# Three mixtures of experts routed by tiles of one expert, with results sent to the tokens' rows

## The reference

```python
# layer 0: two experts a token; h has 512 columns, even ones gate, odd ones linear
t = x * rsqrt(mean(x*x) + 1e-5) * norm_scale
top_v, top_i = top_k(t @ gate_w + gate_b, 2);  probs = softmax(top_v)
h = swiglu(t @ w1[e] + b1[e]);  y = h @ w2[e] + b2[e]      # 128 -> 512 -> 256 -> 128
out = x + sum over e of w[:, e] * y
# layer 2: two experts a token, weights taken from the softmax over all eight
h = gelu(x @ W1[e] + b1[e]);  y = h @ W2[e] + b2[e]         # 128 -> 512 -> 128
# layer 3: one expert a token, the one with the nearest centroid
xn = rms_norm(x) * scale;  a, g = split(xn @ up_w[e])
y = (a * silu(g)) @ down_w[e];  out = y + x                  # 128 -> 512 -> 256 -> 128
```

## Time and profile before

| | us |
|---|---|
| median of 3 runs (lowest, highest) | 4087.44 (4083.16, 4087.86) |
| the profiled execution | 4092.16 |
| its span, first to last instruction | 4090.2 |
| busy in the span: PE, DVE, ACT, POOL | 3379.1, 2559.2, 2091.9, 1303.2 |

### The profile page before, as it was taken

The page is one execution under the profiler, slowest core; times in us unless marked ns, Lnnn a source line. Parts: engine busy times, 40 slices in busy tenths (PEclk is TensorE's granted clock), DMA queues, the critical chain, the costliest instruction groups (busy, mean ns, idle before and its releaser), DMA issues. The chain is left out here.

```text
span 4090.2 us, 79250 instructions
## 1 busy us (share of the span) xinstructions
PE 3379.1 (83%) x30561; PEld 2308.1 (56%) x30561; DVE 2559.2 (63%) x6887; ACT 2091.9 (51%) x3789; POOL 1303.2 (32%) x893
## 2 busy tenths in 40 slices
PE   2999999788999879898999998565468999979742
PEld 1677776556566556664555555343345777656542
DVE  6788888556788679676565554698453222269623
ACT  2677776444555547555555554544175444447521
POOL 3554544122222225203455544232120000015344
PEclk8999999999999989899999999777788999989777
DMA  4333333121000010000000000000420000000012
GB/s 124 53 57 54 53 56 50 51 83 42 1 1 1 1 58 2 1 1 1 2 2 2 2 2 2 6 19 24 135 74 7 1 1 1 1 32 2 5 44 65
DMA packets 74212, 114.31 MB, mean 28 GB/s; under 512 B 19692, under 2 KB 56766, under 8 KB 72446
## 3 DMA queue, kind: packets, MB, share of 16 engines
q1 hardware_dynamic: 71356, 104.89, 10.5%
q0 software_dynamic: 2048, 4.20, 0.4%
q10 hardware_dynamic: 434, 0.15, 0.0%
HBM read 62.45 MB, written 30.47 MB: 23 GB/s over the span
## 5 line engine op out<-in xcount | busy, mean ns | idle before, releaser
L856 PE MATMUL banks<-XT,weight_region 128*128 128x512 f32 x1184 | 549.2, 600 | 1.4 <-DVE T L1231 1.4
L878 PEld LDWEIGHTS banks<-weight_region,HT 128*128 128x128 f32 x3648 | 437.1, 192 | 98.5 <-issue 79.9
L878 PE MATMUL banks<-weight_region,HT 128*128 128x128 f32 x3648 | 442.2, 275 | 6.4 <-ACT HT L1013 5.9
L1254 DVE SCALAR_TENSOR_TENSOR x_res<-banks,WT,x_res 128x128 f32<-128x128 f32 x544 | 153.0, 344 | 405.1 <-PE banks L878 365.8
L856 PEld LDWEIGHTS banks<-XT,weight_region 128*128 128x128 f32 x1184 | 212.7, 193 | 194.2 <-issue 191.4
L1008 ACT ACTIVATE HT<-banks,weight_region 128x512 f32<-128x512 f32 x256 | 173.3, 687 | 239.7 <-PE banks L856 233.5
L458 DVE TENSOR_REDUCE MX<-banks 128x8 f32<-128x1152 f32 x128 | 173.2, 1353 | 103.7 <-PE banks L275 103.6
L1071 POOL TENSOR_TENSOR FNM<-FNM,FRS 128x8 f32<-128x8 f32 x12 | 2.4, 203 | 666.6 <-ACT FRS L967 666.6
L2284 POOL TENSOR_TENSOR SM<-SM,RZ 128x1232 f32<-128x1232 f32 x64 | 143.9, 2249 | 188.4 <-DVE RZ L2326 187.3
L384 ACT COPY PT<-banks 128x384 f32<-128x384 f32 x384 | 170.3, 478 | 48.9 <-PE banks L285 45.0
L285 PE MATMUL banks<-sb_c_ident,SM 128*128 128x128 f32 x1152 | 183.3, 286 | 9.8 <-ACT PT L384 9.4
(11 more groups left out here) (550 smaller groups left out, 8403.7 us busy)
## 6 DMA issues: line engine op xcount, KB each, us to landing
FL<-RAW SPq DMA_DIRECT2D x512, 64.0 KB, 2.3
sorted_rows<-in_zeros_dram SPq DMA_DIRECT2D x33, 512.0 KB, 8.2
T<-s4d_k_dram SPq DMA_DIRECT2D x8, 1024.0 KB, 9.3
weight_region<-in_l_ffn__w_dram SPq DMA_DIRECT2D x3, 2048.0 KB
film_dram<-F SPq DMA_DIRECT2D x8, 512.0 KB, 2.9
FO<-film_dram SPq DMA_DIRECT2D x8, 512.0 KB, 4.3
weight_region<-in_l_ffn__wall_dram SPq DMA_DIRECT2D x1, 3072.0 KB, 10.2
XR<-sorted_rows SPq DMA_DIRECT2D x39, 64.0 KB, 1.8
```

The source lines that it names most:

```text
L856: nc.tensor.matmul(PS[:, q % 4, :], w, xt, start=True, stop=True).then_inc(s.h_ps, 1)
L878: ins = nc.tensor.matmul(PS[:, 4 + u % 2, b * P:(b + 1) * P], HT[:, u % 2, j, b * P:(b + 1) * P], w2[j], start=j == 0, stop=j == len(w2) - 1)
L1254: ins = nc.vector.scalar_tensor_tensor(R[:, t, :], PS[:, 4 + u % 2, b * P:(b + 1) * P], WT[:, t, e:e + 1], R[:, t, :], ALU.mult, ALU.add)
```

## The change

`l0_ffn` and `l2_ffn` now call `routed` too, with two rows a token (K = 2); `l3_ffn` keeps K = 1. `routed` itself is rewritten in these places:

- The number of tiles is 71 for K = 2 and 39 for K = 1. All of them always run.
- A row in `sorted_rows` has 132 numbers instead of 128: the token, the number of its row in the result buffer, and its weight. ScalarE writes these rows into `SRC`, once for each choice (`source`). GpSimd scatters 64 times 128 rows for K = 2, 32 times for K = 1.
- Eight row buffers (LD), and four for staged weights (WB). A register load fetches eight table entries at once (`held`), on SP and on each engine that copies weights.
- Who copies weights: ScalarE all 768 numbers in `l3_ffn`; ScalarE 516 and GpSimd 256 in `l0_ffn`; GpSimd 516 and VectorE 512 in `l2_ffn`.
- The result of a tile is multiplied by the row's weight as it is copied out, and one `DMA_INDIRECT` of GpSimd (`send`) scatters its 128 rows to the tokens' rows in `expert_results`; padding rows go to dummy rows. VectorE works out where (`destination`). SP stores nothing in the loop.
- The bias of the second product no longer enters in the tile loop; it is added to `x_res` in the front (`spread`, `bias`, `base`).
- The tail has no gathers. SP waits for all sends, then loads eight groups of results in token order with plain DMAs (512 KB each for K = 2, 256 KB for K = 1). For K = 2 GpSimd adds the two results of a token, then VectorE adds to `x_res`.
- In the front the rank products of a pair (`ranks`) come before the logits of the next pair; before, they came after.
- The buffer of sorted rows is zeroed as before, in rows of 132.

```diff
+ROW = 132
+RESULTS = 2 * ROWS + (2 * B_ALL + 8) * P
...
+    LD, WB, ST, HELD = 8, 4, 4, 8
+    FAR = float(1 << 20)
+    copies = {"gated": {"act": (0, STAGED)}, "gelu": {"pool": (0, FIRST), "dve": (FIRST, STAGED)},
+              "swiglu": {"act": (0, FIRST), "pool": (FIRST, STAGED)}}[kind]
...
+        def held(eng, table, j, top):
+            n = min(HELD, NT - j)
+            regs = [eng.alloc_register(f"held{nc.next_id()}") for _ in range(n)]
+            eng.load(regs, table[0:1, j:j + n])
+            return [eng.snap(r, donate=True, min_val=0, max_val=top) for r in regs]
+
+        def expert(e, part):
+            return W.wall.rearrange("p e n -> p (e n)")[:, bass.ds(e * STAGED + part[0], part[1] - part[0])]
...
+                sp.wait_ge(s.tab, 1)
+                at = held(nc.sync, RWI, 0, SORTED - P)
+                sp.wait_ge(E.moved, MOVED + 16 * K * NB)
+                for j in range(NT):
+                    if j >= LD:
+                        sp.wait_ge(s.t_ps, j - LD + 1)
+                        sp.wait_ge(s.dst, j - LD + 1)
+                        if K == 2:
+                            sp.wait_ge(s.y_sb, j - LD + 1)
+                    sp.dma_start(XR[:, j % LD, :], rows[bass.ds(at[j % HELD], P), :]).then_inc(loads[j % LD], 16)
+                    if (j + 1) % HELD == 0 and j + 1 < NT:
+                        at = held(nc.sync, RWI, j + 1, SORTED - P)
+                for o in range(ST):
+                    sent(sp, o, len(range(o, NT, ST)))
+                took = results[0:K * ROWS].rearrange("(k p t) d -> p k (t d)", k=K, p=P)
+                for g in range(NG):
+                    sp.dma_start(G[:, g], took[:, :, g * GT:(g + 1) * GT]).then_inc(fetched[g], 16)
...
-                def fetch(j):
-                    if j >= LD:
-                        sp.wait_ge(s.t_ps, j - LD + 1)
-                    r = nc.sync.value_load(ROWI[0:1, j:j + 1], min_val=0, max_val=SORTED - P)
-                    sp.dma_start(XR[:, j % LD, :], rows[bass.ds(r, P), :]).then_inc(loads[j % LD], 16)
-
-                def put(j):
-                    r = nc.sync.value_load(ROWI[0:1, j:j + 1], min_val=0, max_val=SORTED - P)
-                    sp.wait_ge(s.y_sb, j + 1)
-                    sp.dma_start(rows[bass.ds(r, P), :], Y[:, j % ST, :]).then_inc(stores[j % ST], 16)
-
-                sp.wait_ge(s.tab, 1)
-                sp.wait_ge(E.moved, 16 * KTOP * NB)
-                for j in range(NT + LEAD):
-                    if j < NT:
-                        fetch(j)
-                    if j >= LEAD:
-                        put(j - LEAD)
...
+                def rows_out(j):
+                    act.wait_ge(s.y_ps, j + 1)
+                    if j >= ST:
+                        sent(act, j % ST, j // ST)
+                    nc.scalar.activation(Y[:, j % ST, :], down_bank(j), ACT.Identity, scale=XR[:, j % LD, P + 1:P + 2]).then_inc(s.y_sb, 1)
...
-                def bring(g):
-                    for b in range(GB):
-                        t = g * GB + b
-                        for k in range(KTOP):
-                            nc.gpsimd.indirect_dma_start(out=G[:, k, t, :], out_offset=None, in_=rows,
-                                                         in_offset=bass.IndirectOffsetOnAxis(ap=IDX[:, k, t:t + 1], axis=0),
-                                                         bounds_check=SORTED - 1, oob_is_err=False).then_inc(gathers[g], 16)
...
+                def send(j):
+                    pool.wait_ge(s.dst, j + 1)
+                    pool.wait_ge(s.y_sb, j + 1)
+                    nc.gpsimd.indirect_dma_start(out=results, out_offset=bass.IndirectOffsetOnAxis(ap=DST[:, j % ST:j % ST + 1], axis=0),
+                                                 in_=Y[:, j % ST, :], in_offset=None,
+                                                 bounds_check=RESULTS - 1, oob_is_err=False).then_inc(stored[j % ST], 16)
+
+                def both_results(g):
+                    pool.wait_ge(fetched[g], 16)
+                    nc.gpsimd.tensor_tensor(G[:, g, 0], G[:, g, 0], G[:, g, 1], ALU.add).then_inc(s.pairs, 1)
...
+                for j in range(NT + 2):
+                    if "pool" in copies and j < NT:
+                        if j % HELD == 0:
+                            es = held(nc.gpsimd, EJI, j, NE - 1)
+                        stage(j, es[j % HELD])
+                    if j >= 2:
+                        send(j - 2)
+                if K == 2:
+                    for g in range(NG):
+                        both_results(g)
...
+                def base(gp):
+                    for g in (2 * gp, 2 * gp + 1):
+                        dve.wait_ge(s.b2_ps, g + 1)
+                        dve.wait_ge(s.src, g + 1)
+                        if rms:
+                            nc.vector.scalar_tensor_tensor(grp(R, g), grp(R, g), 2.0, PS[:, 7, :].rearrange("p (b d) -> p b d", b=GB),
+                                                           ALU.mult, ALU.add).then_inc(s.base, 1)
...
+                def destination(j):
+                    dve.wait_ge(loads[j % LD], 16 * (j // LD + 1))
+                    if j >= ST:
+                        sent(dve, j % ST, j // ST)
+                    nc.vector.tensor_scalar(DST[:, j % ST:j % ST + 1], XR[:, j % LD, P:P + 1], AWAY[:, j:j + 1], DUMP[:, j:j + 1],
+                                            ALU.add, ALU.min).then_inc(s.dst, 1)
+
+                def columns(j):
+                    dve.wait_ge(s.t_ps, j + 1)
+                    if j >= 2:
+                        dve.wait_ge(s.h_ps, 2 * (j - 1))
+                    nc.vector.tensor_copy(XC[:, j % 2, :], turned(j)).then_inc(s.xs, 1)
+
+                def stage(j, e):
+                    if j >= WB:
+                        dve.wait_ge(s.y_ps, j - WB + 1)
+                    a, b = copies["dve"]
+                    nc.vector.tensor_copy(WR[:, j % WB, a:b], expert(e, (a, b))).then_inc(s.copy_dve, 1)
...
+                for j in range(NT + 3):
+                    if j < NT:
+                        if "dve" in copies:
+                            if j % HELD == 0:
+                                es = held(nc.vector, EJI, j, NE - 1)
+                            stage(j, es[j % HELD])
+                        if not rms:
+                            columns(j)
+                    if 1 <= j <= NT:
+                        if kind == "swiglu":
+                            clip(j - 1)
+                        destination(j - 1)
+                        if kind != "gelu":
+                            gate(j - 1)
+                    if j >= 2 and j - 2 < NT and kind != "swiglu":
+                        rows_out(j - 2)
...
-def l0_ffn(nc, E, **kw): moe(nc, E, "swiglu", **kw)
+                        final_shift(g - 1)
+
+    E.moved_before = MOVED + 16 * K * NB
+    E.stored_before = [n + 16 * len(range(o, NT, ST)) for o, n in enumerate(SENT)]
+
+
+def l0_ffn(nc, E, **kw): routed(nc, E, "swiglu", **kw)
 def l1_ffn(nc, E, **kw): moe(nc, E, "silu", **kw)
-def l2_ffn(nc, E, **kw): moe(nc, E, "gelu", **kw)
+def l2_ffn(nc, E, **kw): routed(nc, E, "gelu", **kw)
```

More of the change, by code:

```diff
@@ L3836, in decoder @@
         run("l2_ffw", l2_close, fo_dram=fo_dram, prefetch=experts)
[L3837 removed]
+        run("l2_ffn", l2_ffn, rows=sorted_rows, results=expert_results, prefetch=place(["l3_attn", "l3_xattn"], REGION - B_ALL * P))
         run("l3_attn", l3_attn)
         run("l3_xattn", l3_xattn, prefetch=place(["l3_ffn"], 0, 10542))
[L3840 removed]
+        run("l3_ffn", l3_ffn, store=out, rows=sorted_rows, results=expert_results)
 def layout(i):
```

460 lines of the change are left out of this document (272 added, 188 removed).

## The result

The changed kernel took 3758.96 us in the median of four runs (3757.22 to 3760.01), the kernel before 4085.3 beside it: a ratio of 0.9204, 95% interval 0.9188 to 0.9220. The forecast was 3747. The profiled execution took 3759.3, its span is 3757.5; the forecast for it was 3752.

A forecast was written before the change was run, and what follows sets the result against it. TensorE alone was taken to bound both dense mixtures, waits for row loads `l3_ffn`'s loop. Fronts, loops and tails gave -88, -178 and -74, together -340: 4092.2 - 340 = 3752 profiled, 3747 for the median; range 3660 to 3865.

The forecast's parts named there:

- TensorE's time of a tile: Tile loops: 0.115 us per 128 columns, so 1.96 us a tile in `l2_ffn`, 1.50 in `l0_ffn` and `l3_ffn`.
- The third rival: Sends beside VectorE's copies take five times 0.62 us; `l2_ffn` tile 4.4 us, 142 us more, 3889; chance 0.05.
- the fourth: GpSimd's 341 indirect DMAs cost more than 1.28 us each; at 2.7, 444 us more, 4191; chance 0.03.
- `l2_ffn`'s loop: Tile loop of `l2_ffn`: 71 tiles at 2.4 us plus 3 to drain, 173 us.
- the lock: `l2_ffn` loop: VectorE's copy and GpSimd exclude each other, adding 0.43 us to GpSimd's 1.88 a tile.
- `l0_ffn`'s loop: Tile loop of `l0_ffn`: 71 tiles at 2.1 us plus 3 to drain, 152 us.
- 0.2 for waits among four engines: `l0_ffn` loop: 0.2 us a tile for waits, added to 1.75 + 0.14, as four engines are all above 1.5.
- my second rival: Loops bound by a round trip among four engines, 2.73 us a tile, 106 us more, 3853; chance 0.16.
- `l3_ffn`'s loop: Tile loop of `l3_ffn`: 39 tiles at 1.76 us (ScalarE's 1.62 + 0.14 for register loads) plus 3, 72 us.
- the first rival: Tile loops run at the busiest engine without added waits, 62 us less than forecast, 3685; chance 0.10.
- Tails: After the last send, loads, sums, root and scalings: 31 us for K = 2, 24 us for K = 1.
- the forecast's own list: Signs of a wrong forecast: sends over 1.3 us, TensorE awaiting weights' copies, VectorE held at `destination`, router behind scatters.

The follow-up runs named there:

- e11: Changed kernel with weight copies one tile further ahead, before the send, and register loads one by one in `l0_ffn` and `l2_ffn`: 3668.38 us, 0.8981 of before.
- e9: Changed kernel with each send one tile later, three tiles behind the copy instead of two, copies left in place: 3674.70 us, 0.8989 of before.

## Why the prediction was right, and where only its sum was

The time was in the range, 12 us above the forecast in the median: 7 of them in the profiled execution (3759.3 against 3752), the rest because it was no longer than the median this time, where the forecast had taken off 4.7. But three terms of the sum were wrong by more than 10 us, two one way and one the other.

- **TensorE's time of a tile** held: 1.45 in `l3_ffn` (forecast 1.50) and, once the circle is open, 1.90 in `l2_ffn` (1.96).
- **Sends**: right. 181 sends took 964/978/988 ns (min/median/max), 160 scatters 972 in the median and 1291 at most, scatters 1.28 us apart, landing in 2.2 and 2.3. The third rival, starved sends, and the fourth, slower than before, are gone by that. In the changed kernel only two sends of `l2_ffn` ran beside VectorE's copy for more than 0.1 us, so it tests the third little; in e11 62 of 71 did, by 0.15 us in the median, and took 992 ns at most. The longest of all, 1.23 us in e9, started 0.06 us into such a copy. The Trainium skill (SBUF — State Buffer, "A bandwidth-pool intuition that's wrong (but worth ruling out)", not the section that the prediction names) has some 3.1 us for its probe beside such a copy; these traces don't show that.
- **`l2_ffn`'s loop**, 2.4 forecast, 2.57 measured: the number was near and its reason false. The step that failed is "if GpSimd waits for it, its period is 1.88 + 0.43". GpSimd wasn't the bound (117 of 186 us busy), and the lock costs 0.10. What stands in its place is the circle, 5.14 us for two tiles in the mean of four pairs.
- **`l0_ffn`'s loop**, 2.1 forecast, 2.31 measured: the term that failed is the "0.2 for waits among four engines", a flat allowance where a way around had to be added up. Its parts were all in hand but one, the 0.84 us from a result to its send. The round trip was my second rival, with 0.16, but I took its price from the old loop of `l3_ffn` (2.73) and not from the queue: I had shown in the order's rows that a send follows each copy on GpSimd, and not asked whose result that send waits for. With the circle open the steady tile takes 1.60, so ScalarE's 1.75 and VectorE's 1.7 to 1.9 were too high as well: they are sums of lengths, and the instructions overlap at their ends.
- **`l3_ffn`'s loop**, 1.76 forecast, 1.45 measured (12 us too many): the sum of ScalarE's instructions, 1.62, counted their ends as if they didn't overlap (it was busy 53.8 us for 39 tiles, 1.38 each), and 0.14 for register loads isn't on the path. Here no copy stands behind a send, since ScalarE copies, and what happened is the first rival, the busiest engine, only that TensorE was it.
- **Fronts**: 108, 103 and 65 forecast, 105.6, 101.7 and 61.7 measured. Most of each is GpSimd's scatters, as said: 80.7, 81.1 and 39.8 us from first to last.
- **Tails**: 31, 31 and 24 forecast, 31.3, 31.1 and 30.2 measured. The term "4.19 MB at 200 GB/s, 21 us" was wrong: the loads went at up to 390 GB/s at a DMA share of 1.

```profile
1292.00:1296.00 4.00, 0.00 (x0) 0.00 (x0) 0.00 (x0) 0.00 (x0) 0.90 (x1) 0.50 0.92 298
1296.00:1300.00 4.00, 0.00 (x0) 0.00 (x0) 3.48 (x15) 0.50 (x2) 3.52 (x3) 0.50 1.04 390
1300.00:1304.00 4.00, 0.00 (x0) 0.00 (x0) 3.86 (x15) 2.65 (x8) 3.99 (x4) 0.50 0.96 357
```

  Not the data but the norms pace the tails. In `l3_ffn` the groups come 2.04 us apart, and ScalarE fills that time with the two steps of a root (0.30 and 0.20) and four scalings (1.54 to the next group's start). It is busy 12.06 of 12.25 us, VectorE 11.40:

```profile
3738.05:3750.30 12.25, 0.00 (x0) 0.00 (x0) 11.40 (x61) 12.06 (x37) 0.00 (x0) 0.50 0.37 140
```

  Eight groups are 16.3 us, where I had 10.5 for the data. For two experts a token a group takes 3.0 us while GpSimd sums (VectorE's sum 0.68, statistics 0.87, means 0.38, and the small operation held for 1.06), then 2.0 to 2.4. From VectorE's first sum to its last small operation these are 20.1 us in `l0_ffn`, and by chance the wrong term had 21.

So the forecast had two loops too short, by 16 and 13 us, and one too long by 12; the fronts (7 less), the tails (7 more) and the 2991.5 us of the rest (9 less) together came out 10 us less than forecast, in part by chance. What the forecast's own list would have shown as wrong did show it: TensorE waiting for a weights' copy, 13 times in `l0_ffn` by name, and 24 times under the name of `XC`.

## What to carry to other kernels

Before you price a loop by its busiest engine, go through each in-order queue and ask, for every instruction that waits, what stands behind it and who needs that; follow it until you are back where you started, and divide the length by the tiles it spans. If an instruction that only needs old data (a copy of weights) stands behind one that needs new data (a send of a result), swap them: here that was worth 85 us of 3759, more than half of what routing `l2_ffn` brought. A waiter's named releaser is a hint; count the rows to see which of its semaphores came last.
